# Scores of a 64-wide attention: three products of float16 halves in place of one float32 product

## The chip, the cores and the metric

The kernel runs on one core of a Trainium2 chip. Its time is device time in microseconds from start to end of one execution, the median of three runs. The core has a matrix engine (TensorE, PE in the trace; its weight loads are the rows PEld), a vector engine (VectorE, DVE), a scalar engine (ScalarE, ACT), GpSimd (POOL) and SyncE (SP), which starts DMA transfers. Each engine takes its own instructions strictly in order; between engines they wait for each other with semaphores. PE writes its results to PSUM, and DVE and ACT read them from there.

## The reference, cut to what matters

The program is a chain of eight stages on a tensor of 16 batch rows of 512 tokens with 128 features. The change lies in the seventh stage alone, an attention with 16 heads of width 64 on the layer-normalised input, whose result is added to the input:

```python
def _L1_attn_b_ref(x, Wq, Wk, Wv, Wo, bo, q_scale, k_scale):
    ...
    q = _l2norm(q) * q_scale
    k = _l2norm(k) * k_scale
    attn = jnp.einsum('bhid,bhjd->bhij', q, k) * DH ** (-0.5)
    attn = jax.nn.softmax(attn, axis=-1)
    out = jnp.einsum('bhij,bhjd->bhid', attn, v)
    out = out.transpose(0, 2, 1, 3).reshape(b, n, H * DH)
    return jnp.einsum('bne,de->bnd', out, Wo) + bo
```

q and k are the projections of x, each head's row brought to length 1; the two scales are inputs with values around 1.

## The kernel before, in words

The function `wide_attention` walks the 16 batch rows one after the other. A batch row has 16 heads, taken in pairs: Q = 0 to 7 is a pair. For a pair the scores are a matrix of 512 keys by 2 x 512 queries, in four units of 128 keys; u is the unit's number, 32 units in a batch row. The step list is one generator, `schedule`, which all engines walk; each engine executes its part of every step in that order. Each Q has three places, A, B and C:

- A: S of units 4Q and 4Q+1; bench steps of place A; SUM(Q, 0); PV and R of the pair before.
- B: bench steps of place B; S of units 4Q+2 and 4Q+3; Z of the pair before.
- C: bench steps of place C; SUM(Q, 1) and SUM(Q, 2).

What the steps do:

- S (L3856): PE multiplies the turned keys `kT` with the turned queries `qT`, for the two heads of the pair at once, one in the upper and one in the lower 64 rows of the array, into one half of the PSUM tile `slot`. ACT takes the exponential of it to `prob` (L3968). A unit's S waits until the exponential of the unit two before is done.
- SUM (L4038): DVE adds up the four units of `prob`. PV (L3870): PE multiplies `prob` with the values. R (L3881): PE sums `sums` over the keys. Then ACT works out an inverse in two instructions (L3944 and L3946), and DVE refines and applies it in three (Z: L4049, L4050, L4052).
- TURN(c) (L3842): PE turns the normalised q and k of pair c (two groups of four 128 x 128 transposes) into two PSUM banks, `bench` 0 for q and `bench` 1 for k. Before the change DVE copies q to `qT` (L4033), and ACT multiplies k by `kw`, which holds the product of both scales, into `kT` (L3959). PE may write a bench bank again only when its reader is done.

The eight TURNs of the next batch row stand at places 5B, 5C, 6A, 6B, 6C, 7A, 7B and 7C. QK (L3816, the projections of q and k of the next row), the squares (L4004) and the norms (L4019) stand in Q = 1 to 4. V (the projection of the values; copies L3952 on ACT and L4026 on DVE) stands at 0B, 0C and 1A, the layer norm's statistics (LN_STATS, L186 and following) and rows (LN_ROWS, L198) on DVE in Q = 0, and Y (L3890, the output projection, added to X at L4058 and L4059) at 1B. All of this shares the two bench banks.

The first batch row is prepared in a part of its own (`first_part`: loads, weights turned, its q and k); its last six TURNs come as a burst at its Q = 0, place A. Batch rows 1 to 14 run in a hardware loop; the last has no row after it to prepare.

## Time and profile before

| | |
|---|---|
| time, median of three runs | 5605.33 us (5605.23 to 5605.4) |
| span of the profiled execution | 5817.8 us |
| its mean granted PE clock | 0.916 |
| PE busy | 4867.1 us (84%) |
| DVE busy | 3629.7 us (62%) |
| ACT busy | 3333.5 us (57%) |
| POOL busy | 1360.1 us (23%) |
| the changed stage, 3711 to 5420 us | PE 1660.06, DVE 1249.13, ACT 1017.50 us busy of 1709.00 |
| scores' matrix products (L3856) | 2048 records, 509.5 us busy |

The profiled execution has only its span as its own time; it is 212 us longer than the median of the runs without the profiler. A row of the trace gives the start, the duration, and in square brackets the idle time of the engine before the row with what ended it. Rows that follow on each other are merged (x8 is eight records). A float32 matrix product with 512 columns leaves two records, a float16 or bfloat16 one leaves one.

### The profile page before, as it was taken

To read this page: it belongs to the slowest core of one execution; us is meant where nothing else is said; L and a number is where in the kernel's file an instruction comes from. 1 tells how busy PE (TensorE), PEld (TensorE's weight loads), DVE (VectorE), ACT (ScalarE), POOL (GpSimd) and SP (SyncE) were. 2 spreads that over 40 slices of the span, in tenths; PEclk is the share of its full clock that TensorE was granted. 3 is DMA by queue.
4 is the path that set the end of the run, shared out by engine and by line. 5 is a ranking of instruction groups with operands and counts; after the bars stand their busy time and mean duration, and the time that the engine had idled before them with its cause. 6 is when DMAs were issued, how large, how long until landed. Compare 5 with 4: busy or idle time off the path is not lost. (4 is left out here: it accounts for less than half of the span.)

```text
span 5817.8 us, 93955 instructions
## 1 busy us (share of the span) xinstructions
PE 4867.1 (84%) x29648; PEld 2462.7 (42%) x29648; DVE 3629.7 (62%) x7303; ACT 3333.5 (57%) x5317; POOL 1360.1 (23%) x1406
## 2 busy tenths in 40 slices
PE   6999768559989967868888659799999999999578
PEld 2222268524444436842222246344344344344255
DVE  5344453477777775347777761576776776776750
ACT  6999644425555544447888722555665665655422
POOL 1111045424334405532323045000000000000055
PEclk8999879869999988989999876899999999999777
DMA  3222121213333312132323232200000000000222
GB/s 83 65 65 63 42 56 39 62 57 91 87 94 91 88 49 60 40 92 51 66 50 66 56 67 43 48 1 0 0 0 0 0 0 0 0 0 0 70 43 40
DMA packets 228016, 265.41 MB, mean 46 GB/s; under 512 B 36874, under 2 KB 194410, under 8 KB 221352
## 3 DMA queue, kind: packets, MB, share of 16 engines
q1 hardware_dynamic: 184180, 194.46, 12.6%
q0 software_dynamic: 43520, 66.97, 6.4%
q8 instruction: 170, 2.79, 0.2%
q14 instruction: 146, 1.20, 0.1%
HBM read 163.86 MB, written 96.65 MB: 45 GB/s over the span
## 5 line engine op out<-in xcount | busy, mean ns | idle before, releaser
L3968 ACT ACTIVATE prob_wide<-slot_wide 128x1024 f32<-128x1024 f32 x512 | 497.2, 1026 | 181.9 <-PE slot_wide L3856 181.9
L2184 ACT ACTIVATE prob_decay<-slot_decay 128x640 f32<-128x640 f32 x512 | 358.8, 705 | 343.8 <-PE slot_decay L2031 342.5
L1000 ACT ACTIVATE prob_rms<-slot_rms 128x1024 f32<-128x1024 f32 x512 | 503.9, 1090 | 56.5 <-PE slot_rms L834 54.0
L2518 DVE TENSOR_TENSOR slot_decay<-slot_decay,dtab_decay 128x512 f32<-128x512 f32 (+3 forms) x1024 | 454.1, 494 | 130.0 <-PE slot_decay L2010 109.9
L1000 ACT ACTIVATE prob_relative<-slot_relative 128x1024 f32<-128x1024 f32 x512 | 497.8, 1049 | 42.1 <-PE slot_relative L834 40.6
L3856 PE MATMUL slot_wide<-qT_wide,kT_wide 64*128 64x512 f32 x2048 | 509.5, 616 | 8.0 <-ACT prob_wide L3968 8.0
L3300 POOL DMA_INDIRECT xg_choice_b<-xn_rows_choice_b,ids_choice_b x64 | 61.1, 955 | 1910.1 <-DVE ids_choice_b L3570 1891.5
L3870 PE MATMUL obank_wide<-prob_wide,v_wide 128*64 128x512 f32 x2048 | 467.7, 598 | 15.3 <-issue 11.6
L1373 DVE TENSOR_TENSOR prob_relative<-prob_relative,rtab_relative 128x1024 f32<-128x1024 f32 (+1 forms) x256 | 394.9, 1548 | 134.9 <-ACT prob_relative L1000 126.7
L3944 ACT ACTIVATE rinv_wide<-rbank_wide 128x512 f32<-128x512 f32 x128 | 76.4, 597 | 481.2 <-PE rbank_wide L3881 481.2
L4038 DVE TENSOR_TENSOR sums_wide<-sums_wide,prob_wide 128x1024 f32<-128x1024 f32 x256 | 312.8, 1222 | 15.0
L858 PE MATMUL obank_relative<-prob_relative,vaug_relative 128*32 128x512 f32 x2048 | 276.0, 611 | 39.7 <-DVE prob_relative L1373 38.1
L3856 PEld LDWEIGHTS slot_wide<-qT_wide,kT_wide 64*128 64x128 f32 x2048 | 174.8, 186 | 263.3 <-issue 200.9
L858 PE MATMUL obank_rms<-prob_rms,vaug_rms 128*32 128x512 f32 x2048 | 274.8, 609 | 2.4 <-ACT osb_rms L1009 1.8
L3870 PEld LDWEIGHTS obank_wide<-prob_wide,v_wide 128*64 128x64 f32 x2048 | 139.0, 136 | 311.6 <-issue 274.9
L2025 PE MATMUL slot_decay<-qst_decay,kst_decay 128*128 128x512 bf16 (+3 forms) x1024 | 226.4, 303 | 34.1 <-DVE slot_decay L2518 32.5
L2010 PE MATMUL slot_decay<-qst_decay,kin_decay 128*128 128x512 bf16 (+3 forms) x1024 | 225.9, 303 | 31.1 <-ACT prob_decay L2184 13.8
L3816 PE MATMUL bench_wide<-wT_wide,xnT_wide 128*128 128x512 f32 x492 | 243.8, 618 | 0.8 <-ACT xnT_wide L3911 0.8
L834 PE MATMUL slot_rms<-qst_rms,kst_rms 64*128 64x512 bf16 x1024 | 195.1, 391 | 33.8 <-DMA kst_rms<-scratch_rms 29.1
L834 PE MATMUL slot_relative<-qst_relative,kst_relative 64*128 64x512 bf16 x1024 | 193.1, 391 | 16.5 <-DMA qst_relative<-no_shift_relative 10.9
L2050 PE MATMUL obank_decay<-prob_decay,vaug_decay 128*32 128x512 f32 (+3 forms) x2048 | 191.4, 446 | 0.8 <-ACT prob_decay L2184 0.8
L834 PEld LDWEIGHTS slot_rms<-qst_rms,kst_rms 64*128 64x128 bf16 x1024 | 46.4, 93 | 312.6 <-ACT prob_rms L1000 158.7
(861 smaller groups left out, 10385.7 us busy)
## 6 DMA issues: line engine op xcount, KB each, us to landing
scratch_decay<-parts_decay SPq DMA_DIRECT2D x192, 128.0 KB, 2.4
qst_decay<-scratch_decay SPq DMA_DIRECT2D x128, 128.0 KB
scratch_rms<-parts_rms SPq DMA_DIRECT2D x96, 128.0 KB
kst_rms<-scratch_rms POOLq DMA_DIRECT2D x96, 128.0 KB, 5.5
kst_decay<-scratch_decay SPq DMA_DIRECT2D x192, 64.0 KB
kin_decay<-scratch_decay SPq DMA_DIRECT2D x192, 64.0 KB
scratch_relative<-parts_relative SPq DMA_DIRECT2D x96, 128.0 KB
kst_relative<-scratch_relative POOLq DMA_DIRECT2D x96, 128.0 KB, 6.2
```

Of the source, the lines that this page charges most:

```text
L834: last = nc.tensor.matmul(slot[:, u % 3, k * S:k * S + m], kst[half_rows(k), buffer[0], pair, kb * P:(kb + 1) * P], qst[half_rows(k), buff ...
L858: last = nc.tensor.matmul(obank[32 * j:32 * j + 32, c0:c1], vaug[:, vp, kb, head(g, j), :], prob[:, Q % 2, j, at + c0 - q0:at + c1 - q0], ...
L1000: nc.scalar.activation(prob[:, Q % 2, p:G:2, at:at + m], slot[:, u % 3].rearrange("p (k c) -> p k c", k=2)[:, :, 0:m], ACT.Exp).then_inc(e ...
L1373: last = nc.vector.tensor_tensor(v, v, of_group(rtab, g)[:, :, :, c0:c0 + (hi - lo) * P], ALU.mult)
L2025: last = nc.tensor.matmul(slot[:, u % 3, at:at + m], kst[:, h, kb * P:(kb + 1) * P], qst[:, h, q0:S], start=not decay, stop=not decay, ski ...
L2184: nc.scalar.activation(prob[:, Q % 2, j, 0:c1 - c0], slot[:, u % 3, c0:c1], ACT.Exp).then_inc(exp_done, 1)
L2518: last = nc.vector.tensor_tensor(sl, sl, dtab[:, h, 0:m], ALU.mult)
L3816: nc.tensor.matmul(qk_bank(b, 4 * t + j), xnT[:, t * P:(t + 1) * P], wT[:, j // 2, (j % 2) * S:(j % 2 + 1) * S], start=True, stop=True).th ...
L3856: last = nc.tensor.matmul(slot[:, u % 2, hh * S:(hh + 1) * S], kT[r, Q, kb * P:(kb + 1) * P], qT[r, Q, :], start=True, stop=True)
L3870: nc.tensor.matmul(obank[W * hh:W * hh + W, :], v[:, kb, (2 * Q + hh) * W:(2 * Q + hh + 1) * W], prob[:, Q % 2, kb, hh * S:(hh + 1) * S], ...
L3968: nc.scalar.activation(prob[:, Q % 2, u % 4, :], slot[:, u % 2, :], ACT.Exp).then_inc(exp_done, 1)
L4038: add = nc.vector.tensor_tensor(sums[:, Q % 2, :], first, prob[:, Q % 2, i + 1, :], ALU.add)
```

## The change

The turned q and k are kept as pairs of float16 numbers: a high part (the value rounded) and a low part (what the rounding left). A score is then the sum of three float16 products, low k with high q, high k with low q, and high k with high q, which are accumulated in PSUM. To stay in float16's range q is multiplied by 2^14, and k by its scale divided by the largest scale; the exponential gives both back through its scale operand.

On ACT each TURN now issues two instructions (q high, k high) where it issued one, and on DVE two (q low, k low), each after the high part that it subtracts, where it issued one. PE may write a bench bank again after the low part. PE issues six matrix products a unit where it issued two. The start has two more loads of 1024 scales, broadcast to all partitions, and seven DVE instructions that find the largest.

```diff
--- before.py
+++ after.py
@@ -3582,6 +3582,8 @@
     W = 64
     C = H * W // P
     FIRST_TURNS = 2
+    HALF_MAX = 2.0 ** 14
+    PRODUCTS = ((1, 0), (0, 1), (0, 0))
     ctx = ExitStack()
     with ctx:
         def sb(name, shape, dt=F32):
@@ -3602,8 +3604,10 @@
         qk = sb("qk", [P, TPB, 2, H * W])
         sq = sb("sq", [P, 2, H * W])
         ss = sb("ss", [P, 3, TPB * 2 * H])
-        kT = sb("kT", [P, C, S])
-        qT = sb("qT", [P, C, S])
+        kT = sb("kT", [P, 2, C, S], F16)
+        qT = sb("qT", [P, 2, C, S], F16)
+        peak = sb("peak", [P, 2])
+        kinv = sb("kinv", [P, 1])
         v = sb("v", [P, TPB, H * W])
         ones = sb("ones", [P, W])
         prob = sb("prob", [P, 2, TPB, 2 * S])
@@ -3622,6 +3626,7 @@
         qk_filled, qk_drained, qk_ready = sem("qk_filled"), sem("qk_drained"), sem("qk_ready")
         squared, sq_read = sem("squared"), sem("sq_read")
         turn_filled, q_turned, k_turned = sem("turn_filled"), sem("q_turned"), sem("k_turned")
+        q_high, k_high = sem("q_high"), sem("k_high")
         v_filled, v_low, v_high = sem("v_filled"), sem("v_low"), sem("v_high")
         s_filled, exp_done, r_done, z_ready = sem("s_filled"), sem("exp_done"), sem("r_done"), sem("z_ready")
         summed = sem("wide_summed")
@@ -3632,13 +3637,16 @@
 
 
         raw = prob[:].rearrange("p a b c -> p (a b c)")
+        all_scales = [sums[:, i] for i in range(2)]
         QR = 3 * C * D
         sources = [(raw[:, i * C * D:(i + 1) * C * D].rearrange("p (c i) -> p c i", i=D),
                     A[w[name]].rearrange("(c o) i -> o c i", o=P)) for i, name in enumerate(("wq", "wk", "wv"))]
         first_loads = [(ident[:], const(A, "ident"))] + sources[0:2]
         loads = [sources[2], (raw[:, QR:QR + H * W], A[w["wo"]]),
                  (scales[:, 0, :], A[w["qs"]].rearrange("(c a) o d -> c (a o d)", a=2)),
-                 (scales[:, 1, :], A[w["ks"]].rearrange("(c a) o d -> c (a o d)", a=2)), (bo_t[:], rows(A[w["bo"]]))]
+                 (scales[:, 1, :], A[w["ks"]].rearrange("(c a) o d -> c (a o d)", a=2)), (bo_t[:], rows(A[w["bo"]])),
+                 (all_scales[0], rows(A[w["qs"]].rearrange("h o d -> (h o d)"))),
+                 (all_scales[1], rows(A[w["ks"]].rearrange("h o d -> (h o d)")))]
 
         HALVES_AT = {(1, "C"): (0, 0), (2, "A"): (0, 1), (2, "B"): (1, 0), (2, "C"): (1, 1), (3, "A"): (2, 0),
                      (3, "B"): (2, 1), (3, "C"): (3, 0), (4, "A"): (3, 1)}
@@ -3851,10 +3859,13 @@
                             pe.wait_ge(k_turned, b * C + (Q + 1))
                         if u >= 2 or not at_start(b, 0):
                             pe.wait_ge(exp_done, b * UNITS + (u - 1))
-                        for hh in range(2):
-                            r = slice(W * hh, W * hh + W)
-                            last = nc.tensor.matmul(slot[:, u % 2, hh * S:(hh + 1) * S], kT[r, Q, kb * P:(kb + 1) * P],
-                                                    qT[r, Q, :], start=True, stop=True)
+                        for i, (kp, qp) in enumerate(PRODUCTS):
+                            for hh in range(2):
+                                r = slice(W * hh, W * hh + W)
+                                last = nc.tensor.matmul(
+                                    slot[:, u % 2, hh * S:(hh + 1) * S], kT[r, kp, Q, kb * P:(kb + 1) * P],
+                                    qT[r, qp, Q, :], start=(i == 0), stop=(i == len(PRODUCTS) - 1),
+                                    skip_group_check=True)
                         last.then_inc(s_filled, 1)
                     if step == "PV":
                         Q = a[0]
@@ -3926,7 +3937,8 @@
                         for m in range(4, C):
                             keep_weights(m)
                         act.wait_ge(setup_pe, C + 1)
-                        nc.scalar.copy(kw[:], obank[:, 0:C]).then_inc(setup_act, 1)
+                        act.wait_ge(setup_dve, 2)
+                        nc.scalar.activation(kw[:], obank[:, 0:C], ACT.Copy, scale=kinv[:, 0:1]).then_inc(setup_act, 1)
                         act.wait_ge(setup_act, C + 1)
                     if step == "LNEXP":
                         t = a[0]
@@ -3955,9 +3967,12 @@
                         m = n if later else b
                         if not at_start(m, 0):
                             act.wait_ge(s_filled, (m - 1) * UNITS + 4 * (c + 1))
+                        act.wait_ge(turn_filled, m * (2 * C) + (2 * c + 1))
+                        nc.scalar.activation(qT[:, 0, c, :], bench[:, 0, :], ACT.Copy, scale=HALF_MAX
+                                             ).then_inc(q_high, 1)
                         act.wait_ge(turn_filled, m * (2 * C) + (2 * c + 2))
-                        nc.scalar.activation(kT[:, c, :], bench[:, 1, :], ACT.Copy, scale=kw[:, c:c + 1]
-                                             ).then_inc(k_turned, 1)
+                        nc.scalar.activation(kT[:, 0, c, :], bench[:, 1, :], ACT.Copy, scale=kw[:, c:c + 1]
+                                             ).then_inc(k_high, 1)
                     if step == "S":
                         u = a[0]
                         Q = u // 4
@@ -3965,7 +3980,8 @@
                         if not (at_start(b, 0) and Q < 2):
 
                             act.wait_ge(r_done, b * C + (Q - 1))
-                        nc.scalar.activation(prob[:, Q % 2, u % 4, :], slot[:, u % 2, :], ACT.Exp).then_inc(exp_done, 1)
+                        nc.scalar.activation(prob[:, Q % 2, u % 4, :], slot[:, u % 2, :], ACT.Exp, scale=peak[:, 1:2]
+                                             ).then_inc(exp_done, 1)
                 nc.scalar.preload_act_table_set("natural_log_exp_and_others")
                 for m in range(4):
                     keep_weights(m)
@@ -3998,6 +4014,15 @@
                             nc.vector.scalar_tensor_tensor(out=scales[:, 0, :], in0=scales[:, 0, :], scalar=W ** -0.5,
                                                            in1=scales[:, 1, :], op0=ALU.mult, op1=ALU.mult
                                                            ).then_inc(setup_dve, 1)
+                            link(nc.vector.tensor_tensor(all_scales[0], all_scales[0], all_scales[1], ALU.mult))
+                            link(nc.vector.reduce_max(peak[:, 0:1], all_scales[0], AX_X))
+                            link(nc.vector.tensor_reduce(out=peak[:, 1:2], in_=all_scales[0], op=ALU.min, axis=AX_X))
+                            link(nc.vector.scalar_tensor_tensor(out=peak[:, 0:1], in0=peak[:, 1:2], scalar=-1.0,
+                                                                in1=peak[:, 0:1], op0=ALU.mult, op1=ALU.max))
+                            link(nc.vector.tensor_scalar(peak[:, 0:1], peak[:, 0:1], W ** -0.5 / HALF_MAX, 1e-30,
+                                                         ALU.mult, ALU.max))
+                            nc.vector.tensor_scalar(peak[:, 1:2], peak[:, 0:1], 1.0 / HALF_MAX, None, ALU.mult)
+                            nc.vector.reciprocal(kinv[:], peak[:, 0:1]).then_inc(setup_dve, 1)
                     if step == "SQUARES":
                         t, i = a
                         dve.wait_ge(squared, n * (4 * TPB) + (4 * t + 2 * (i + 1)))
@@ -4029,8 +4054,14 @@
                         m = n if later else b
                         if not at_start(m, 0):
                             dve.wait_ge(s_filled, (m - 1) * UNITS + 4 * (c + 1))
-                        dve.wait_ge(turn_filled, m * (2 * C) + (2 * c + 1))
-                        nc.vector.tensor_copy(qT[:, c, :], bench[:, 0, :]).then_inc(q_turned, 1)
+                        dve.wait_ge(q_high, m * C + (c + 1))
+                        nc.vector.scalar_tensor_tensor(out=qT[:, 1, c, :], in0=bench[:, 0, :], scalar=HALF_MAX,
+                                                       in1=qT[:, 0, c, :], op0=ALU.mult, op1=ALU.subtract
+                                                       ).then_inc(q_turned, 1)
+                        dve.wait_ge(k_high, m * C + (c + 1))
+                        nc.vector.scalar_tensor_tensor(out=kT[:, 1, c, :], in0=bench[:, 1, :], scalar=kw[:, c:c + 1],
+                                                       in1=kT[:, 0, c, :], op0=ALU.mult, op1=ALU.subtract
+                                                       ).then_inc(k_turned, 1)
                     if step == "SUM":
                         Q, i = a
                         dve.wait_ge(exp_done, b * UNITS + (4 * Q + i + 2))
```

VectorE's rows at pair Q = 7 before the change (`qT` is the turned q, `rfix` and `zT` are Z, `sums` is SUM):

```order
L4033 COPY qT_wide<-bench_wide 128x512
L4049 TENSOR_TENSOR rfix_wide<-rbank_wide,rinv_wide 128x512
L4050 SCALAR_TENSOR_TENSOR rfix_wide<-rfix_wide,rinv_wide 128x512
L4052 SCALAR_TENSOR_TENSOR zT_wide<-obank_wide,rfix_wide 128x512
...
L4033 COPY qT_wide<-bench_wide 128x512
...
L4038 TENSOR_TENSOR sums_wide<-sums_wide,prob_wide 128x1024
```

And after it, at the same place:

```order
L4058 SCALAR_TENSOR_TENSOR qT_wide<-bench_wide,qT_wide 128x512
L4062 SCALAR_TENSOR_TENSOR kT_wide<-bench_wide,kw_wide,kT_wide 128x512
L4080 TENSOR_TENSOR rfix_wide<-rbank_wide,rinv_wide 128x512
L4081 SCALAR_TENSOR_TENSOR rfix_wide<-rfix_wide,rinv_wide 128x512
L4083 SCALAR_TENSOR_TENSOR zT_wide<-obank_wide,rfix_wide 128x512
...
L4058 SCALAR_TENSOR_TENSOR qT_wide<-bench_wide,qT_wide 128x512
L4062 SCALAR_TENSOR_TENSOR kT_wide<-bench_wide,kw_wide,kT_wide 128x512
...
L4069 TENSOR_TENSOR sums_wide<-sums_wide,prob_wide 128x1024
```

The first TURN's two parts now stand ahead of Z, and the second's ahead of the sums.

ScalarE's rows behind an R in the turning pairs, before the change (`rinv` is the inverse, `prob` the exponential):

```order
L3944 ACTIVATE rinv_wide<-rbank_wide 128x512
L3946 ACTIVATE rinv_wide<-rinv_wide 128x512
L3959 ACTIVATE kT_wide<-bench_wide,kw_wide 128x512
...
L3968 ACTIVATE prob_wide<-slot_wide 128x1024
```

And after it:

```order
L3956 ACTIVATE rinv_wide<-rbank_wide 128x512
L3958 ACTIVATE rinv_wide<-rinv_wide 128x512
L3971 ACTIVATE qT_wide<-bench_wide 128x512
L3974 ACTIVATE kT_wide<-bench_wide,kw_wide 128x512
...
L3983 ACTIVATE prob_wide<-slot_wide,peak_wide 128x1024
```

The high part of q, which is new on this engine, stands behind the two instructions of the inverse.

## Rows read from the trace of the kernel before

**Rows 1.** Busy time in two stretches: PE, PEld, DVE, ACT, POOL, granted clock, DMA.

```profile
3711.00:5420.00 1709.00, 1660.06 (x7336) 692.50 (x7338) 1249.13 (x1808) 1017.50 (x1567) 0.00 (x0) 1.00 0.00 0
2700.00:3280.00 580.00, 509.55 (x3462) 156.49 (x3460) 449.35 (x494) 510.57 (x669) 165.17 (x155) 1.00 0.25 55
```

**Rows 2.** Instructions by line: busy, mean ns | idle before, and its releaser.

```profile
L3856 PE MATMUL slot_wide<-qT_wide,kT_wide 64*128 64x512 f32 x2048 | 509.5, 616 | 8.0 <-ACT prob_wide L3968 8.0
L3959 ACT ACTIVATE kT_wide<-bench_wide,kw_wide 128x512 f32<-128x512 f32 x128 | 87.2, 681 | 12.4 <-PE bench_wide L3842 12.4
```

**Rows 3.** PE in order of time, one batch row: start, us, instruction [idle].

```profile
4241.36 1.09 PE L3842 MATMUL bench_wide<-ident_wide,qk_wide 128*128 128x128 f32 x8
...
4264.34 3.65 PE L3870 MATMUL obank_wide<-prob_wide,v_wide 128*64 128x512 f32 x16 [0.83 <-issue]
...
4326.06 1.08 PE L3881 MATMUL rbank_wide<-sums_wide,ones_wide 128*64 128x512 f32 x4 [1.43 <-DVE sums_wide L4038]
...
4338.42 1.09 PE L3842 MATMUL bench_wide<-ident_wide,qk_wide 128*128 128x128 f32 x8
4339.44 1.99 PE L3856 MATMUL slot_wide<-qT_wide,kT_wide 64*128 64x512 f32 x8
4341.36 1.09 PE L3842 MATMUL bench_wide<-ident_wide,qk_wide 128*128 128x128 f32 x8
...
4345.32 3.65 PE L3870 MATMUL obank_wide<-prob_wide,v_wide 128*64 128x512 f32 x16
4348.81 1.03 PE L3881 MATMUL rbank_wide<-sums_wide,ones_wide 128*64 128x512 f32 x4
4349.77 0.44 PE L3842 MATMUL bench_wide<-ident_wide,qk_wide 128*128 128x128 f32 x2
```

**Rows 4.** DVE in order of time, the same batch row.

```profile
4248.12 0.86 DVE L186 BATCH_NORM_STATS2 stats_wide<-X 128x6 f32 x4
...
4254.01 0.69 DVE L4026 COPY v_wide<-bench_wide 128x512 f32<-128x512 f32 x1 [0.22 <-DVE sums_wide L4038]
...
4257.81 0.68 DVE L4026 COPY v_wide<-bench_wide 128x512 f32<-128x512 f32 x1
...
4276.83 0.69 DVE L4058 TENSOR_TENSOR X<-X,bo_t_wide 128x512 f32 x1 [11.46 <-PE bench_wide L3890]
...
4290.03 0.69 DVE L4049 TENSOR_TENSOR rfix_wide<-rbank_wide,rinv_wide 128x512 f32<-128x512 f32 x1 [2.94 <-ACT rinv_wide L3946]
...
4339.11 0.69 DVE L4033 COPY qT_wide<-bench_wide 128x512 f32<-128x512 f32 x1 [3.46 <-PE bench_wide L3842]
4339.83 0.69 DVE L4049 TENSOR_TENSOR rfix_wide<-rbank_wide,rinv_wide 128x512 f32<-128x512 f32 x1
...
4342.09 0.69 DVE L4033 COPY qT_wide<-bench_wide 128x512 f32<-128x512 f32 x1
4342.70 2.56 DVE L4038 TENSOR_TENSOR sums_wide<-sums_wide,prob_wide 128x1024 f32<-128x1024 f32 x2
```

**Rows 5.** ACT in order of time, pair Q = 6.

```profile
4338.53 0.60 ACT L3944 ACTIVATE rinv_wide<-rbank_wide 128x512 f32<-128x512 f32 x1 [3.71 <-PE rbank_wide L3881]
4339.16 0.63 ACT L3946 ACTIVATE rinv_wide<-rinv_wide 128x512 f32<-128x512 f32 x1
4339.70 0.67 ACT L3959 ACTIVATE kT_wide<-bench_wide,kw_wide 128x512 f32<-128x512 f32 x1
```

**Rows 6.** 16-bit products of other stages, in order of time.

```profile
300.58 0.39 PE L834 MATMUL slot_rms<-qst_rms,kst_rms 64*128 64x512 bf16 x2
300.90 1.06 PE L858 MATMUL obank_rms<-prob_rms,vaug_rms 128*32 128x512 f32 x8
...
1509.39 0.43 PE L2025 MATMUL slot_decay<-qst_decay,kst_decay 128*128 128x384 bf16 x2
1509.66 0.27 PE L2031 MATMUL slot_decay<-negb_decay,identb_decay 128*128 128x128 bf16 x2
```

**Rows 7.** DVE subtracts a bfloat16 part in the first stage: min/median/max ns.

```profile
L1318 DVE SCALAR_TENSOR_TENSOR rest_rms<-bench_rms,kw_rms,parts_rms x15: 750/751/751, 72.7 to 608.0; 128x512 f32<-128x512 f32 x15
```

**Rows 8.** DVE at the stage's start: the first squares.

```profile
3677.43 1.22 DVE L4004 TENSOR_REDUCE ss_wide<-sq_wide 128x16 f32<-128x1024 f32 x1 [4.71 <-ACT sq_wide L3923]
```

## The prediction

> **What bounds the kernel now.** I read the stretches first. In the changed stage PE is busy 1660 of 1709 us, 97%, at a granted clock of 1.00; DVE is at 73% and ACT at 60% [rows 1]. PE sets the pace, so work taken off PE should shorten the stage. The scores hold 509.5 us of it [rows 2], and that is what the change wants to cut.
>
> An average over the stage hides that its parts differ, so I then read one batch row in order of time on PE. It begins for me with the turn at place 7B, at 4241.36, and the same step of the next row stands at 4349.77: a batch row takes 108.4 us, and the stage has sixteen. PE has three idle spots in it that matter [rows 3]: 0.83 us ahead of the first PV, which waits for DVE's copy of v, and 1.43 us ahead of R of pair 4, which waits for DVE's sums. So at Q = 2 to 4 it is DVE, full of squares and norms, that comes last. On DVE the long waits are 11.46 us for Y, 2.94 us for the inverse at pair 1 and 3.46 us for a turn [rows 4]; between 4290 and 4326 its answer shows no wait at all. Hence three kinds of stretch: PE-bound with DVE near (the turns at Q = 5 to 7), mixed (Q = 0), DVE-bound (Q = 2 to 4).
>
> **What PE saves.** Two units of scores now take 4341.36 - 4339.44 = 1.92 us [rows 3]. With float16 they are six passes of 512 columns, the two heads of a pair side by side in the two halves of the array. Two bfloat16 products one behind the other, of 384 and 256 columns (together they fill a score tile of 640), take 1509.66 - 1509.39 = 0.27 us, and 640 columns at 2.4 GHz are 0.267 us: one column a cycle, with the weight loads hidden. A 64-row pair with 512 columns between other work takes 300.90 - 300.58 = 0.32 us, 0.213 for its columns and 0.107 for getting started [rows 6]. So two units become 6 x 0.213 + 0.107 = 1.39 us: 0.53 saved, 256 times, 136 us in all, if nothing else comes last. The bound from the other side is that each pair costs the whole 0.32: 6 x 0.32 = 1.92, nothing saved. I take 1.39, as the row of back-to-back products shows the very case of two products in a row.
>
> **What the turns cost.** The terms are these. ACT issues q high and k high; k's copy took 0.68 [rows 2], I take the same for both, 0.60 from start to start. DVE issues q low and k low. The nearest row subtracts a bfloat16 part from PSUM in 0.75 us [rows 7], against 0.69 for the copy that goes; a DVE instruction of this size lets an independent one start after 0.61 (4342.70 - 4342.09) and one that depends on it after 0.72 (4339.83 - 4339.11) [rows 4]. I take 0.64 from start to start and 0.75 to the end. By count, 128 turns add about 85 us to ACT and 104 us to DVE, which would be 70% and 86% of a stage of 1573 us. That is no bound by itself, but the order matters: the low part waits for the high part, the high part of q stands behind the inverse on ACT, and two more instructions stand ahead of Z and of the sums on DVE.
>
> Walk one turning pair, Q = 6, with time 0 where PE starts TURN B (4338.42). Before: TURN 1.02, scores 1.92, TURN, scores, TURN 1.02 each, PV 3.49, R 0.96, 11.35 in all, without idle time [rows 3].
> - ACT: inverse at 0.11 and 0.74, free at 1.28 [rows 5]; q high 1.28 to 1.96, k high 1.88 to 2.56.
> - DVE: q low 2.00 to 2.75, k low from 2.64 to 3.39; Z from 3.30, and the next from 5.56 (Z took 4342.09 - 4339.83 = 2.26, [rows 4]).
> - PE: TURN B to 1.02, scores to 2.41, TURN C from about 2.85 (q low B done), its k half after 3.5, done at 4.0; scores to 5.4. TURN A of the next pair needs bench 0 back, which q low C reads from 5.56 to 6.25: it starts at 6.37, idle for 1.0 us; its k half waits for k low C, which is done at 6.95, and ends at 7.58. PV to 11.07, R to 12.03.
> - The sums follow k low C, 6.87 to 9.3, so R isn't late; q low A, k low A and the first sum end at 11.9, before the next turn's q low. The pattern repeats.
>
> So a turning pair takes 12.05 us where it took 11.35: 0.7 longer though PE has 1.07 less to do. PE's saving turns into idle time before its bench banks. There are two such pairs in a batch row (5B to 6B, 6B to 7B): +1.4.
>
> From 7B to the end of R of pair 0 (4241.36 to 4264.34 + 4.45, 27.43 us [rows 3]): the two turns make DVE reach the layer norm's statistics at 9.32 instead of 4248.12 - 4241.36 = 6.76, 2.55 late, and all behind it moves: the high half of v(0) is copied at 15.2 (was 12.65), that of v(1), behind the layer norm's rows, at 19.0 (was 16.45) [rows 4]. PE comes to v(0) at 10.5, to v(1) at 13.8, but its second half needs bench 1 from the first copy, 16.0; v(2)'s second half needs it from the second copy, 19.8. Then scores 20.8 to 22.2, v(3) to 24.1, PV at 25.07, R done at 29.5: +2.1.
>
> Behind it Y waits for PE only, and DVE's 11.46 us take up the shift. From Y to R of pair 1 PE saves two pairs of units, 1.06 us: DVE's wait of 2.94 shrinks to 1.9. From there to R of pair 4 DVE has no wait, so the other scores of Q = 2 to 5 save nothing: -1.06 for the whole of Q = 1 to 5A.
>
> **The sum.** A batch row: 1.4 + 2.1 - 1.06 = +2.4. Fifteen rows turn (15 x 1.4 = 21), fourteen have the long Q = 0 behind turns (14 x 2.1 = 29), fifteen gain 1.06 (-16). The last row prepares nothing, PE alone bounds it: 16 x 0.53 less what it inherits, -7. The six turns in a burst at row 0: each cycle through bench 0 is PE 0.51, 0.18 to the reader, 0.68, 0.75, 0.12, about 2.2 instead of 1.5 us (an estimate from the same rows), +4; the two before it, in series, +2. The start: seven DVE instructions, three of them over 1024 elements at 1.22 [rows 8], 4.5 us, behind 1 MB more of loads; DVE had 4.71 us of idle time there, so +3, bounds 0 and +8. Together 21 + 29 - 16 - 7 + 6 + 3 = +36 us, on the profiled span of 5817.8 us as on the median of 5605.3, since PE's clock in this stage is at its upper level already and nothing in it is DMA: 5641 us.
>
> The exponential's scale from a column may cost what k's copy pays over a plain one, under 0.1 us; ACT waits for PE in most places, so nothing. The clock: PE will be busy some 89% of the stage. In the fifth stage it is busy 509.55 of 580 us, 88%, and granted 1.00 [rows 1]: I expect no fall.
>
> One rule speaks against the change. First the rows: R of pair 4 waits 1.43 us for DVE's sums [rows 3], and DVE's last wait before it ended at 4290.03 [rows 4]; that place is bound by DVE, which empties PSUM. The Trainium skill, "TensorEngine Tiling (Array Packing)", section "PSUM Bottleneck", says that making TensorE faster by tiles doesn't speed up the emptying of PSUM, which may then become the bound. By it alone the saving would be lost and the sum would end at no change or above; the trace agrees at pairs 2 to 4, and at the turns only once the second reader is added.
>
> **The rivals.**
> 1. PE's work is what counts, 16%: the walk's delays overlap better than I give them, so that the turning pairs take PE's own 10.28 (-1.07 each) and Q = 0 too keeps its two savings (-2.1), with -1.06 at Q = 1 to 5. For: 97% busy PE. Against: banks can't be given back before the low part. 15 x (-5.3) - 8 + 9 = -79: 5526 us. Half of it would be 5565.
> 2. A wash, 13%: the low parts cost 0.6 each and DVE's lateness at Q = 0 vanishes in its small waits; then 21 x 0.5 + 0 - 16 - 7 + 9 is about 0: 5605 us.
> 3. The float16 pairs don't stream, 10%: 0.32 each. Then the scores take as long as before; the turning pairs stay at 12.05, as idle time covers it, Q = 0 costs 0.5 more, Q = 1 to 5 gain nothing, nor the last row: 36 + 16 + 7 + 7 = +66: 5671 us.
> 4. The clock drops in the stage, 4%, for stretches of it: a loss beyond +80.
> My forecast has 57%: 5641, own range 5612 to 5680, since each of the three terms may be off by a third and the walk by 0.5 us a row in each.
>
> **How the numbers follow.** What a measurement can tell is about 0.2%, 11 us: 5594 to 5616. Slower holds nearly all of the forecast, the third and the fourth case, 0.70; same the second and the forecast's edge, 0.13; faster the first and part of the second, 0.17. The range leaves the full first case out below and the clock above: 5585 to 5695.
>
> **What would show it.** Right: scores of two units 1.39 us apart in the new trace; PE idle about 1 us before the q half of TURN A at pairs 6 and 7, released by DVE's q low; idle of over 1 us inside v(1) and v(2); idle before R of pairs 2 to 4 grown from 1.43; a batch row of about 110.8 us. Wrong: a batch row under 108 us would mean that the drains are shorter or overlap more than I walked; scores at 1.92 would mean the third rival; low parts far from 0.75 us the second or worse; a granted clock below 1.00 between 3750 and 5400 us the fourth.

## The result, and the profile after

The changed kernel takes 5639.41 us (median of four runs, 5637.23 to 5642.25), the kernel before 5605.28 us beside it. The ratio is 1.0065, with a 95% interval of 1.005 to 1.0079: slower by 34 us, 28 to 44. The forecast was 5641.

The profiled execution of the changed kernel has a span of 5638.9 us. That of the kernel before has 5817.8, and the difference lies in stages that the change doesn't touch: the changed stage begins at 3660.86 us there and at 3490.53 here. So I compare the changed stage by its pieces and not the spans. From its first VectorE instruction to the last batch row's output row (`X<-X,bo_t`, L4058 before and L4089 after) it takes 1773.0 us before (3660.86 to 5433.86) and 1813.3 us after (3490.53 to 5303.78).

Busy time and granted clock in a stretch of the changed stage (columns as in [rows 1]):

```profile
3600.00:5280.00 1680.00, 1521.38 (x8125) 629.50 (x8126) 1284.43 (x1858) 1067.33 (x1631) 0.00 (x0) 0.99 0.00 0
```

PE is down from 97% to 91%, DVE up from 73% to 76%, ACT from 60% to 64%. PE has less to do and the stage is 40 us longer: what grew is PE's idle time.

Instructions by line, which answer to [rows 2] and [rows 7]:

```profile
L3983 ACT ACTIVATE prob_wide<-slot_wide,peak_wide 128x1024 f32<-128x1024 f32 x512 | 545.1, 1125 | 165.3 <-PE slot_wide L3865 165.3
L3865 PE MATMUL slot_wide<-qT_wide,kT_wide 64*128 64x512 f16 x3072 | 384.4, 381 | 24.1 <-ACT prob_wide L3983 23.0
L4062 DVE SCALAR_TENSOR_TENSOR kT_wide<-bench_wide,kw_wide,kT_wide 128x512 f16<-128x512 f32 x128 | 95.0, 742 | 1.7 <-ACT kT_wide L3974 1.7
L4058 DVE SCALAR_TENSOR_TENSOR qT_wide<-bench_wide,qT_wide 128x512 f16<-128x512 f32 x128 | 88.3, 690 | 106.2 <-ACT qT_wide L3971 101.2 <-PE slot_wide L3865 2.7
L3971 ACT ACTIVATE qT_wide<-bench_wide 128x512 f16<-128x512 f32 x128 | 77.7, 607 | 11.6 <-PE bench_wide L3850 11.6
```

The scores' busy time fell from 509.5 to 384.4 us, by 125 us. By the starts of the rows it is 256 times 1.92 - 1.40 = 0.52 us, 133 of the 136 us forecast. The low part of q costs the 0.69 us of the copy that it replaces, that of k 0.74. Ahead of its low part of q DVE now waits for ACT's high part, 101.2 us in all; ahead of the copy before the change it waited for PE's transposes, 126.1 us in all.

PE in order of time, one batch row of the changed kernel; it answers to [rows 3]:

```profile
4099.85 1.98 PE L3840 MATMUL bench_wide<-wT_wide,xnT_wide 128*128 128x512 f32 x4
4101.77 1.47 PE L3865 MATMUL slot_wide<-qT_wide,kT_wide 64*128 64x512 f16 x12
4103.17 1.12 PE L3840 MATMUL bench_wide<-wT_wide,xnT_wide 128*128 128x512 f32 x2
4105.37 1.98 PE L3840 MATMUL bench_wide<-wT_wide,xnT_wide 128*128 128x512 f32 x4 [1.07 <-DVE v_wide L4051]
4109.17 1.12 PE L3840 MATMUL bench_wide<-wT_wide,xnT_wide 128*128 128x512 f32 x2 [1.82 <-DVE v_wide L4051]
...
4118.88 0.66 PE L3813 MATMUL bench_wide<-ident_wide,xn_wide 128*128 128x128 f32 x4
...
4166.10 0.82 PE L3865 MATMUL slot_wide<-qT_wide,kT_wide 64*128 64x512 f16 x6 [0.96 <-ACT prob_wide L3983]
4167.10 0.82 PE L3865 MATMUL slot_wide<-qT_wide,kT_wide 64*128 64x512 f16 x6 [0.18 <-ACT prob_wide L3983]
4169.66 3.65 PE L3881 MATMUL obank_wide<-prob_wide,v_wide 128*64 128x512 f32 x16 [1.74 <-DVE zT_wide L4083]
4175.15 1.08 PE L3892 MATMUL rbank_wide<-sums_wide,ones_wide 128*64 128x512 f32 x4 [1.83 <-DVE sums_wide L4069]
4176.16 1.09 PE L3850 MATMUL bench_wide<-ident_wide,qk_wide 128*128 128x128 f32 x8
...
4182.23 1.31 PE L3850 MATMUL bench_wide<-ident_wide,qk_wide 128*128 128x128 f32 x8 [0.72 <-DVE qT_wide L4058]
...
4187.92 1.09 PE L3850 MATMUL bench_wide<-ident_wide,qk_wide 128*128 128x128 f32 x8
...
4194.18 1.31 PE L3850 MATMUL bench_wide<-ident_wide,qk_wide 128*128 128x128 f32 x8 [0.81 <-DVE qT_wide L4058]
...
4199.87 1.09 PE L3850 MATMUL bench_wide<-ident_wide,qk_wide 128*128 128x128 f32 x8
...
4210.15 1.98 PE L3840 MATMUL bench_wide<-wT_wide,xnT_wide 128*128 128x512 f32 x4
```

The reader is to see four things. Two units of scores are 1.40 us apart (4101.77 to 4103.17). The turning pairs last 11.76 and 11.95 us (4176.16, 4187.92, 4199.87), with PE idle for 0.72 and 0.81 us before TURN A for DVE's low part of q. Inside v(1) and v(2) PE waits 1.07 and 1.82 us for DVE's copy. Ahead of R of pair 4 it waits 1.83 us for the sums where it waited 1.43, another 1.74 ahead of PV for DVE's Z, and 0.96 and 0.18 for exponentials, where one wait of 0.35 stood before. The whole row takes 110.30 us (4099.85 to 4210.15).

### The profile page after: what moved, and what is told of

It is laid out like the page before. It is cut to its first block and busy times, and to the rows that moved or that the text cites. A ratio compares the mean times of both kernels' runs of the same rounds, so it can differ in the third digit from the quotient of the medians.

```text
span 5638.9 us, 96147 instructions
## 1 busy us (share of the span) xinstructions
PE 4649.7 (82%) x30576; PEld 2335.8 (41%) x30672; DVE 3706.3 (66%) x7438; ACT 3416.2 (61%) x5445; POOL 1388.5 (25%) x1406
## 5 line engine op out<-in xcount | busy, mean ns | idle before, releaser
L3983 ACT ACTIVATE prob_wide<-slot_wide,peak_wide 128x1024 f32<-128x1024 f32 x512 | 545.1, 1125 | 165.3 <-PE slot_wide L3865 165.3
L3865 PE MATMUL slot_wide<-qT_wide,kT_wide 64*128 64x512 f16 x3072 | 384.4, 381 | 24.1 <-ACT prob_wide L3983 23.0
L3865 PEld LDWEIGHTS slot_wide<-qT_wide,kT_wide 64*128 64x128 f16 x3072 | 127.8, 95 | 281.0 <-issue 119.8
L2010 PE MATMUL slot_decay<-qst_decay,kin_decay 128*128 128x128 bf16 (+3 forms) x960 | 211.7, 297 | 35.7 <-ACT prob_decay L2184 14.8
L3850 PE MATMUL bench_wide<-ident_wide,qk_wide 128*128 128x128 f32 x1024 | 160.1, 288 | 43.2 <-DVE qT_wide L4058 32.8
```

Source lines behind the costliest of these rows:

```text
L3865: last = nc.tensor.matmul(slot[:, u % 2, hh * S:(hh + 1) * S], kT[r, kp, Q, kb * P:(kb + 1) * P], qT[r, qp, Q, :], start=(i == 0), stop=(i ...
L3983: nc.scalar.activation(prob[:, Q % 2, u % 4, :], slot[:, u % 2, :], ACT.Exp, scale=peak[:, 1:2]).then_inc(exp_done, 1)
```

## The experiments

All were timed beside the kernel before, whose median was 5602.97 us beside one product, no low parts, plain exponential and late layer norm, 5601.92 beside PV first, the two moves and the layer norm in the kernel before, and 5601.46 beside the others. The changed kernel was not timed again; "less than the changed kernel" is against its 5639.41, and since the kernel before moved by 4 us from set to set (5605.28 beside the changed kernel), such a difference is good to about 4 us. Sections of a batch row are: turning pair (TURN B to TURN B), Q = 0, and from R of pair 0 to R of pair 4.

**One product.** Less work for PE, all reads of PSUM kept:

```diff
-    PRODUCTS = ((1, 0), (0, 1), (0, 0))
+    PRODUCTS = ((0, 0),)
```

> The changed kernel with one float16 product a score, high k with high q (the two low products are left out); all reads of the bench banks stay. Two units of scores then take 2 x 0.213 + 0.107 = 0.53 us on PE instead of 1.39, 0.86 us less, 256 times, 220 us. Theory (the turned parts' chain over ACT and DVE sets the turning pairs, DVE the pairs 2 to 4): the turning pairs stay at 11.8 to 12.0 us, Q = 0 gains about 0.4, Q = 1 about 1.7, the last batch row about 13; together some 45 us less than the changed kernel's 5639: 5595, between 5580 and 5610. Rival (PE's work still sets the stage): 5639 - 220 = 5419, or at least half of the 220: 5530 or less.

Measured: 5676.13 us (5655.25 to 5678.64), ratio 1.0131 (1.0116 to 1.0147). Both theories missed the time: with 220 us of matrix work taken away the kernel got slower than the changed one. The profiled execution took 5655.25 us, and the three others 5674.89 to 5678.64, so the trace shows only 16 of the 37 us. PE in order of time shows where, and so does the clock (the column behind POOL):

```profile
3600.00:5280.00 1680.00, 1385.35 (x6116) 549.10 (x6114) 1279.36 (x1856) 1065.18 (x1633) 0.00 (x0) 0.95 0.00 0
```

```profile
4172.09 0.39 PE L3865 MATMUL slot_wide<-qT_wide,kT_wide 64*128 64x512 f16 x2 [1.83 <-ACT prob_wide L3983]
4173.10 0.39 PE L3865 MATMUL slot_wide<-qT_wide,kT_wide 64*128 64x512 f16 x2 [0.61 <-ACT prob_wide L3983]
4175.98 6.00 PE L3881 MATMUL obank_wide<-prob_wide,v_wide 128*64 128x512 f32 x16 [2.49 <-DVE zT_wide L4083]
...
4295.23 1.09 PE L3850 MATMUL bench_wide<-ident_wide,qk_wide 128*128 128x128 f32 x8
...
4306.98 1.09 PE L3850 MATMUL bench_wide<-ident_wide,qk_wide 128*128 128x128 f32 x8
```

Behind waits of 1.83, 0.61 and 2.49 us one PV takes 6.00 us, where it takes 3.65 at 2.4 GHz: it ran mostly at 1.2 GHz. The granted clock of the stretch is 0.95 against 0.99, that is 10% of the time at half speed against 2%. The two effects can be told apart in the trace. The two turning pairs from 4295.23 to 4318.90 ran at a granted clock of 1.00 and take 11.75 and 11.95 us, as in the changed kernel (11.76 and 11.95), though PE has 1.7 us less to do in each: there the theory held. The slow stretches cost more than the other sections saved: a batch row takes 109.1 to 109.5 us or 111.8 to 112.5 where the changed kernel takes 110.30. The opposite was run too.

**Four products.** High k with high q twice, so 109 us more for PE and less idle time:

```diff
-    PRODUCTS = ((1, 0), (0, 1), (0, 0))
+    PRODUCTS = ((1, 0), (0, 1), (0, 0), (0, 0))
```

> The changed kernel with a fourth product a score (high k with high q is added a second time, so the scores are off). Two units of scores take 8 x 0.213 + 0.107 = 1.81 us instead of 1.39, 0.43 more, 256 times, 109 us, and PE waits less, so the clock should have no reason to fall. Theory: the added work goes into PE's waits at the turns and at pairs 2 to 4; a batch row gets 0.4 longer at Q = 0 and 0.9 at Q = 1, 1.4 with the rest, 15 times, and the last row 7, less some 5 to 10 for the low clock that goes: about 15 to 20 more than 5639: 5656, between 5645 and 5675. Rival (PE's work sets the time): 109 more, 5748, or at least half of it, 5694.

Measured: 5654.54 us (5652.0 to 5658.7), ratio 1.0097 (1.0081 to 1.0112). Of 109 us 15 arrive. The granted clock from 3600 to 5250 us is 1.00. The turning pair's wait has taken the work up:

```profile
4178.02 1.09 PE L3850 MATMUL bench_wide<-ident_wide,qk_wide 128*128 128x128 f32 x8
4179.05 1.90 PE L3865 MATMUL slot_wide<-qT_wide,kT_wide 64*128 64x512 f16 x16
...
4184.10 1.31 PE L3850 MATMUL bench_wide<-ident_wide,qk_wide 128*128 128x128 f32 x8 [0.29 <-DVE qT_wide L4058]
...
4189.78 1.09 PE L3850 MATMUL bench_wide<-ident_wide,qk_wide 128*128 128x128 f32 x8
```

The pair still takes 11.76 us, though its scores take 1.83 instead of 1.40; the wait before TURN A is 0.29 instead of 0.72.

**No low parts.** DVE has no part in a TURN, and ACT's high parts give the banks back:

```diff
# ScalarE
-  nc.scalar.activation(qT[:, 0, c, :], ...).then_inc(q_high, 1)
+  nc.scalar.activation(qT[:, 0, c, :], ...).then_inc(q_turned, 1)
-  nc.scalar.activation(kT[:, 0, c, :], ...).then_inc(k_high, 1)
+  nc.scalar.activation(kT[:, 0, c, :], ...).then_inc(k_turned, 1)
# VectorE: the step TURN is left out
-    PRODUCTS = ((1, 0), (0, 1), (0, 0))
+    PRODUCTS = ((0, 0), (0, 0), (0, 0))
```

> The changed kernel without the low parts: DVE has no part in a TURN, ACT's high parts alone give the bench banks back, and the three products all read the high parts (the low parts are left out of the sum), so that PE does the same work. Theory: a turning pair falls from 11.85 to about 10.8 us, as PE waits no more for DVE but at most for ACT; from 7B to the end of R of pair 0 it falls from 29.3 to about 25.8; Q = 1 to 5 stay at 57.2. A batch row 104.6 instead of 110.3, 15 times 5.7 = 85 less: 5554, between 5535 and 5580. Rival (the loss comes from the scores' longer exponential, the scales' setup and the low clock in a few spots, not from the turns): 5630 or more.

Measured: 5553.38 us (5551.87 to 5555.82), ratio 0.991 (0.9895 to 0.9925): 86 us less than the changed kernel, where 85 were worked out. The two agree in part by luck: a batch row falls to 105.17 us and not to 104.6, and what that lacks is made up ahead of the loop, which had not been counted (from the stage's first VectorE instruction to the first output row 178.5 us where the changed kernel has 195.2).

```profile
4143.32 1.09 PE L3850 MATMUL bench_wide<-ident_wide,qk_wide 128*128 128x128 f32 x8
...
4154.04 1.09 PE L3850 MATMUL bench_wide<-ident_wide,qk_wide 128*128 128x128 f32 x8
```

A turning pair takes 10.7 us. The second readers on DVE cost 86 us, more than the 50 us by which the faster products alone beat the kernel before (5602.97 to 5553.38).

**Plain exponential.** A constant in place of the column that gives the scale back:

```diff
-  ... ACT.Exp, scale=peak[:, 1:2]
+  ... ACT.Exp, scale=2.0 ** -28
```

> The changed kernel with a constant in the exponential's scale in place of the column that gives the largest scale back (so the scores are off by a factor). The exponential took 1.125 us with the column and 1.026 without it, 512 times, 51 us of ACT's time. Theory: ACT waits for PE nearly everywhere, so nothing: 5639, between 5632 and 5643. Rival (the longer exponential is part of the loss): 10 to 50 us less, 5590 to 5629.

Measured: 5637.94 us (5637.14 to 5641.95), ratio 1.0063 (1.0049 to 1.0077). No difference to the changed kernel, though the exponential fell to 1038 ns. Nearly all of ACT's 45 us lie beside other work; only in the last batch row a pair gets shorter by them, from 8.64 to 8.45 us, 1 us in all.

**Late layer norm.** The next row's statistics and rows go where DVE waits for Y:

```diff
-  # Q == 0: "LN_STATS" before SUM(0, 0), "LN_ROWS" behind Z
             if Q == 1 and place == "B":
                 if nxt:
-                    yield "TURN_X",
+                    yield "LN_STATS",
+                    yield "LN_ROWS",
                 if prev:
                     yield "Y",
+                if nxt:
+                    yield "TURN_X",
```

> The changed kernel with the next row's layer norm (statistics and rows, 5.5 us of DVE) moved from Q = 0 to place 1B ahead of Y, where DVE sits idle for 11.5 us, and the transpose of x put behind Y on PE. Theory (DVE's lateness behind the turns reaches PE at Q = 0 by the copies of v): both waits of PE inside v(1) and v(2), 1.07 and 1.82 us, go, and R of pair 0 ends about 3 us earlier; 15 rows give 43: 5597, between 5588 and 5610. Rival (those waits only hide others behind them, ACT's copies or Y's): less than 1 us a row, 5625 or more.

Measured: 5597.31 us (5593.5 to 5603.62), ratio 0.999 (0.9981 to 0.9999): 42 us less than the changed kernel. On PE, V in this kernel:

```profile
4196.79 1.98 PE L3839 MATMUL bench_wide<-wT_wide,xnT_wide 128*128 128x512 f32 x4
4200.11 4.10 PE L3839 MATMUL bench_wide<-wT_wide,xnT_wide 128*128 128x512 f32 x8
4205.53 1.98 PE L3839 MATMUL bench_wide<-wT_wide,xnT_wide 128*128 128x512 f32 x4
4208.35 3.65 PE L3880 MATMUL obank_wide<-prob_wide,v_wide 128*64 128x512 f32 x16 [0.83 <-ACT v_wide L3963]
```

v(1) and v(2) run through in 4.10 us. From v(0) to PV there are 11.56 us (4196.79 to 4208.35) where the changed kernel has 14.59 (4099.85 to its PV at 4114.44). A batch row falls from 110.30 to 107.33 us. The move helps only where DVE is late, which the same move in the kernel before shows:

> The kernel before with the layer norm moved to 1B ahead of Y. Theory: there DVE isn't late at Q = 0, PE waits 0.3 us in v(1) and v(2), so the move gives at most 0.3 us a row, 0 to 5 us of 5605. That would show that the gain of the same move in the changed kernel is the turns' lateness taken back. Rival (the layer norm at Q = 0 is a burden of its own): 20 us or more less, 5585 or below.

Measured: 5600.09 us (5597.81 to 5606.76) against 5601.92, ratio 0.9997 (0.9988 to 1.0006): no difference. In the changed kernel the layer norm stood in the way because the turns had made DVE late.

**PV first.** The TURNs of 6A and 7A behind PV:

```diff
-                yield from bench_steps(Q, "A", prev, nxt)
+                late = nxt and (Q, "A") in TURNS_AT
+                if not late:
+                    yield from bench_steps(Q, "A", prev, nxt)
 ...
                     yield "PV", (Q - 1) % C
+                if late:
+                    yield from bench_steps(Q, "A", prev, nxt)
+                if pv:
                     yield "R", (Q - 1) % C
```

> The changed kernel with the TURN of places 6A and 7A put behind PV instead of ahead of it, on all engines, so that PE does 3.5 us of PV while DVE still reads the bench banks. Theory (PE's wait for the second reader of bench 0 is what makes the turning pairs long): the waits of 0.72 and 0.81 us before TURN A go; another of 0.3 may come before TURN B, and DVE's q low then waits less on the inverse. A pair falls from 11.85 to about 11.2, 2 x 0.65 x 15 = 20 us: 5620, between 5610 and 5632. Rival (DVE's and ACT's serial work as such sets the pair, wherever PE waits): no change, 5635 to 5645.

Measured: 5619.82 us (5617.29 to 5621.02), ratio 1.0032 (1.002 to 1.0044): 20 us less than the changed kernel.

```profile
4175.81 1.31 PE L3855 MATMUL bench_wide<-ident_wide,qk_wide 128*128 128x128 f32 x8
...
4178.60 3.65 PE L3886 MATMUL obank_wide<-prob_wide,v_wide 128*64 128x512 f32 x16
4182.19 1.09 PE L3855 MATMUL bench_wide<-ident_wide,qk_wide 128*128 128x128 f32 x8
...
4186.97 1.27 PE L3855 MATMUL bench_wide<-ident_wide,qk_wide 128*128 128x128 f32 x8
```

From TURN C of pair 5 (4175.81) to TURN C of pair 6 (4186.97) are 11.16 us, and no wait for DVE stands before TURN A. DVE's and ACT's work is the same as before the move, so it was where PE waited, and not their total, that made the pair long.

**A part of the sums on PE.** At pairs 2 to 4 DVE adds three units, and R multiplies the ones also with the fourth:

```diff
+    ON_PE = (2, 3, 4)
 # R
+  parts = [sums[:, Q % 2]] + ([prob[:, Q % 2, 3]] if Q in ON_PE else [])
 # schedule
-                yield "SUM", Q, 2
+                if Q not in ON_PE:
+                    yield "SUM", Q, 2
```

> The changed kernel with a part of DVE's sums at pairs 2, 3 and 4 given to PE: DVE adds three of the four units, and R multiplies the ones with the sums and with the fourth unit. It takes 3 x 1.25 us from DVE and adds 3 x 0.96 us to PE in each row, where PE waits about 4.7 us now (0.96, 0.18, 1.74 and 1.83). Theory (DVE bounds pairs 2 to 4, so that what PE saved there was lost): PE's waits there shrink, and the row gets shorter by what PE then has left, 4.7 - 2.9 = 1.8 us, 27 in all: 5612, between 5602 and 5625. Rival (PE bounds it): 2.9 more a row, 43 in all: 5682.

Measured: 5623.41 us (5620.41 to 5628.29), ratio 1.0038 (1.0025 to 1.0052): 16 us less than the changed kernel, where 27 were worked out.

```profile
4118.69 0.66 PE L3815 MATMUL bench_wide<-ident_wide,xn_wide 128*128 128x128 f32 x4
...
4167.63 0.82 PE L3867 MATMUL slot_wide<-qT_wide,kT_wide 64*128 64x512 f16 x6 [0.96 <-ACT prob_wide L3987]
4168.63 0.82 PE L3867 MATMUL slot_wide<-qT_wide,kT_wide 64*128 64x512 f16 x6 [0.18 <-ACT prob_wide L3987]
4169.39 3.65 PE L3883 MATMUL obank_wide<-prob_wide,v_wide 128*64 128x512 f32 x16
...
4175.01 1.09 PE L3852 MATMUL bench_wide<-ident_wide,qk_wide 128*128 128x128 f32 x8
```

PE's two waits for DVE are gone, and R of pair 0 to R of pair 4 takes 56.32 us (4118.69 to 4175.01) instead of 57.28 (4118.88 to 4176.16). The sign is what the theory needs: work moved on to PE made the kernel faster, so DVE did bound these pairs. (R's two rows of `sums` and `prob` stand between the last two lines shown; neither waits.) The size was off because I had counted the waits of 0.96 and 0.18 us among those that go; they are for the exponential, and they stay. What was left is 1.74 + 1.83 less 2.9 of added work, 0.7, and measured is 0.96 a row.

**Two moves, and all three.**

> Both moves at once in the changed kernel: the next row's layer norm at 1B ahead of Y, and the TURNs of 6A and 7A behind PV. If the two places are apart, as the theory has it, their gains add: 43 + 20 = 63 less than 5639: 5576, between 5560 and 5595, faster than the kernel before. Rival (each move only shifts the wait to the same next one): no more than the better of the two alone.

Measured: 5575.36 us (5568.14 to 5579.49), ratio 0.995 (0.9936 to 0.9963): 64 less than the changed kernel, 42 and 20 alone.

> All three moves in the changed kernel: the layer norm at 1B ahead of Y, the TURNs of 6A and 7A behind PV, and the fourth unit's sum at pairs 2 to 4 on PE. Each lies in another part of the batch row, so the gains should add: 5575 - 27 = 5548, between 5535 and 5562. Rival: they share a bound, and the third move adds nothing or costs its PE work, 5575 to 5618.

Measured: 5558.34 us (5558.04 to 5562.88), ratio 0.9926 (0.9912 to 0.9939): 17 less than the two alone, as the third move by itself (16), where 27 had been put into the sum again. It is the full computation, and beats the kernel before by 0.74%. The gains add, so the three places don't share one bound.

## Why the prediction was right, point by point

- **The scores' price.** 1.39 us for two units was forecast, 1.40 measured. Two units as one, three and four products take 0.53, 1.40 and 1.83 us, which is 0.22 us for each further pass of 512 columns (0.213 at one column a cycle of 2.4 GHz): the passes stream with their weight loads hidden. Of the third rival nothing came.
- **The turning pairs.** Forecast 12.05, measured 11.76 and 11.95, from 11.35: +1.0 for both instead of +1.4. The term was mis-sized by 0.1 to 0.3 a pair. ACT's high part of q took 0.61 us and not 0.68, and DVE's low part of q 0.69 and not 0.75, which fits the size; no run tests it. The mechanism is shown by three runs: with one product, at a granted clock of 1.00, the pair stays at 11.75; no low parts brings it to 10.7; PV ahead of TURN A brings it to 11.16.
- **Q = 0.** The prediction has the 0.83 us ahead of the first PV as a wait for DVE's copy of v; its row says `<-issue`, and in the changed kernel the same 0.83 us ends with ACT's copy of v. It is the same in both, so nothing hangs on it. From TURN B at 7B to the end of R of pair 0 the forecast was 29.5 us; measured is 10.28 (4199.87 to 4210.15) and 19.03 (4099.85 to 4118.88), 29.31, from 27.43. The two waits inside v(1) and v(2) were forecast at 1.3 and 1.9 and are 1.07 and 1.82. Moving the layer norm away took them back, and only in the changed kernel.
- **Q = 1 to 5.** Forecast 1.06 saved, measured 58.28 - 57.28 = 1.0. The further scores of pairs 2 to 4 became waits of PE, as forecast; their growth was in a new wait ahead of PV (1.74) more than in the one ahead of R. DVE's wait at pair 1 fell from 2.94 to 1.91. The prediction counts three idle spots of PE and names two; the third is the 0.35 us for the exponential at pair 4 that became 0.96 and 0.18. It also takes these pairs as a case of DVE being late in emptying PSUM. Most of DVE's rows there are squares, norms and sums, which read `sq`, `qk` and `prob` outside PSUM; only Z reads PSUM. So these pairs don't bear out that rule; the turns and the copies of v do.
- **The row and the sum.** Forecast +2.4 a row, measured 110.30 - 108.41 = +1.9. The stage, cut at the output rows, shows where the sum went:

| | before | after | difference | forecast |
|---|---|---|---|---|
| first VectorE instruction to first output row | 182.3 | 195.2 | +12.9 | +11.4 |
| thirteen rows of the loop | 1409.4 | 1437.2 | +27.7 | +31.2 |
| the last two stretches (the last batch row) | 181.3 | 180.9 | -0.4 | -6.7 |
| the stage | 1773.0 | 1813.3 | +40 | +36 |

(The forecast's column puts its terms, 3 + 6 for the start and the burst and 1.4, 2.1 and -1.06 for a row, where they fall.) The clock that I had denied is in the second line: I expected no fall, and a granted clock below 1.00 was my sign for the fourth rival. Eleven of the thirteen rows take 110.29 to 110.31 us and two 111.93 and 111.94 (the two DVE rows below bound one of them, with a granted clock of 0.98): 3.3 us in all. So 0.5 us too much for a row, 7 us over the loop, met errors of the opposite sign: 3 us of clock, 6 us in the last batch row and 1.5 us ahead of the loop; 5641 against 5639 is closer than the working deserves. The stage's +40 is one traced execution of each kernel, and the runs say 34, between 28 and 44.

```profile
4126.92 0.69 DVE L4089 TENSOR_TENSOR X<-X,bo_t_wide 128x512 f32 x1 [11.45 <-PE bench_wide L3901]
4238.85 0.69 DVE L4089 TENSOR_TENSOR X<-X,bo_t_wide 128x512 f32 x1 [11.45 <-PE bench_wide L3901]
```

- **The last batch row.** This is the term of the sum that was furthest off: -7, "PE alone bounds it", and measured is -0.4. A pair of that row takes 8.64 us where it took 8.79, though PE has 1.04 us less to do: its wait for the exponential grew from 0.44 to 1.05, and the scores behind that wait, held up once more inside the group, take 1.74 us where 1.47 is the usual. So ACT's exponentials, and not PE alone, bound it. PE in the changed kernel, and in the kernel before:

```profile
5249.12 1.74 PE L3865 MATMUL slot_wide<-qT_wide,kT_wide 64*128 64x512 f16 x12 [1.05 <-ACT prob_wide L3983]
...
5257.76 1.74 PE L3865 MATMUL slot_wide<-qT_wide,kT_wide 64*128 64x512 f16 x12 [1.05 <-ACT prob_wide L3983]
```

```profile
5380.17 1.99 PE L3856 MATMUL slot_wide<-qT_wide,kT_wide 64*128 64x512 f32 x8 [0.44 <-ACT prob_wide L3968]
...
5388.96 1.99 PE L3856 MATMUL slot_wide<-qT_wide,kT_wide 64*128 64x512 f32 x8 [0.44 <-ACT prob_wide L3968]
```

At its end the low clock takes another 1.7 us: the last PV runs 5.35 us there and 3.65 before the change. Without that the row would give -2.1.

- **The start.** The seven new DVE instructions took from 3504.86 to the first squares at 3509.14, 4.3 us where 4.5 were worked out. The wait for the loads ahead of them (and of the old product of the scales, the first row) was 6.22 us, and 3.68 before the change:

```profile
3504.65 0.28 DVE L4014 SCALAR_TENSOR_TENSOR scales_wide<-scales_wide 8x128 f32<-8x128 f32 x1 [6.22 <-DMA sums_wide<-in_L_attn_b_k_scale]
...
3509.14 2.33 DVE L4029 TENSOR_REDUCE ss_wide<-sq_wide 128x16 f32<-128x1024 f32 x2
...
3532.03 1.97 PE L3850 MATMUL bench_wide<-ident_wide,qk_wide 128*128 128x128 f32 x8 [6.03 <-DVE qk_wide L4044]
...
3541.56 1.22 PE L3850 MATMUL bench_wide<-ident_wide,qk_wide 128*128 128x128 f32 x8 [1.84 <-DVE qT_wide L4058]
3543.69 1.31 PE L3850 MATMUL bench_wide<-ident_wide,qk_wide 128*128 128x128 f32 x8 [0.91 <-DVE qT_wide L4058]
```

The first squares come 18.6 us after the stage's first DVE instruction (3490.53) instead of 16.6 (3660.86 to 3677.43), but the first TURN only 1.1 later (41.5 and 40.4 us after it), where +3 was forecast. The turns of the burst are 2.13 us apart (3541.56 to 3543.69), 2.2 forecast; behind the burst PE is 7.5 us late in all, of 9. Two more pieces make the +12.9 of the table: the first batch row's own Q = 0 is 2.2 us longer (20.5 and 18.3), for which the forecast had nothing, and the second one's 3.5 instead of 2.1, with scores at the low clock in it (one group of 1.47 us takes 2.59).

What stays open is the whole share of the clock in the 34 us. In the loop it is the 3.3 us of two rows; at the start and at the end the granted clock is lower too (0.89 from 3490 to 3685 us against 0.93 over the same part before, 0.95 from 5230 to 5304 against 0.98), and no run held it up there and left all else alone.

## What to carry to other kernels

When a product is split into parts to make the matrix engine faster, count first who empties its PSUM bank, and when the bank comes back: a second reader that waits for the first puts two engines in series at each tile. A busy share of 97% says that an engine sets the pace on average, not that time taken off it is time saved; walk one period and see at each place what comes last. If the walk shows a wait, look for an engine's idle stretch elsewhere in the period (here DVE's 11.5 us before Y) or an independent block to put there (here PV). In this kernel these two moves, and one sum given to PE, turned +0.65% into -0.74%. Walk the periods that differ, too: the last batch row, without turns, waited for another engine than the others and gave nearly none of the 7 us expected of it.

## What the runs showed of the hardware that I had not expected

- A column as the exponential's scale makes it longer: 1125 ns on 128 x 1024 against 1038 with a constant and 1026 without a scale.
- Less work for PE can cost time. With one product in place of three PE was busy 1385 us instead of 1521 in the same stretch of 1680, its granted clock fell from 0.99 to 0.95, and the kernel became 37 us slower by the median (16 in the execution traced). With four products it was 1.00. In the stage before the change, 97% busy, the clock was 1.00 from 3711 to 5420 us, and in the fifth stage, 88% busy, it was 1.00 too [rows 1]; from that row I had expected no fall in the changed stage, at 91% busy, and got 0.99.
